# Phase 1 of a quantized feed-forward kernel: x turned on VectorE in 32x32 squares instead of on TensorE

## What is computed

```python
x: (4, 1024, 512)    cond: (4, 256)    W: (1536, 512)    w1: (2048, 512)    w2: (512, 2048)
hidden   = concat([cond, cond], -1)
fused    = concat([x, mean(x, axis=1) * ones, hidden * ones], -1)       # (4, 1024, 1536)
relation = relu(einsum('bld,do->blo', fused, W) + b)
def quant_linear(v, w, bias):
    s_in = max(max(v), 1e-8) / 255;             vq = clip(round(v / s_in), 0, 255) * s_in
    s_w  = max(max|w| per row, 1e-8) / 127;     wq = clip(round(w / s_w), -128, 127) * s_w
    return vq @ wq.T + round(bias / (s_in * s_w)) * (s_in * s_w)
h   = relu(quant_linear(relation, w1, b1))
out = x + quant_linear(h, w2, b2)
```

## Time and profile before

| | us |
|---|---|
| median of 3 runs | 348.81 (348.67 to 349.97) |
| the profiled execution | 349.05 |
| its span, first to last instruction | 346.8 |
| phase 1, to the first product of phase 2 | 0 to 117.5 |
| phase 2 | 117.5 to about 229 |
| phase 3 | about 233 to 346.8 |

### The profile page before, as it was taken

The page is one execution under the profiler, slowest core; times in us unless marked ns, Lnnn a source line. Parts: engine busy times, 40 slices in busy tenths (PEclk is TensorE's granted clock), DMA queues, the critical chain, the costliest instruction groups (busy, mean ns, idle before and its releaser), DMA issues.

```text
span 346.8 us, 5358 instructions
## 1 busy us (share of the span) xinstructions
PE 337.3 (97%) x1645; PEld 196.2 (57%) x1645; DVE 271.4 (78%) x590; ACT 155.7 (45%) x263; POOL 1.1 (0%) x8
## 2 busy tenths in 40 slices
PE   6999999999999999999999999989999999999996
PEld 5788888888868544444444444434444444444444
DVE  1877668658684789999999999988486595685996
ACT  2635225325412499970000000038959559568800
POOL 1000000000000000000000000000000000000000
PEclk9999999999999999999999999999999999999999
DMA  7965998964432128886781030037984399977116
GB/s 247 404 214 171 325 326 241 285 188 177 121 60 41 21 122 363 346 347 287 323 335 60 0 121 0 0 121 289 402 341 183 133 412 424 361 241 227 78 60 242
DMA packets 29934, 74.90 MB, mean 216 GB/s; under 512 B 17864, under 2 KB 18144, under 8 KB 22496
## 3 DMA queue, kind: packets, MB, share of 16 engines
q1 hardware_dynamic: 29920, 74.73, 59.7%
HBM read 45.37 MB, written 25.17 MB: 203 GB/s over the span
## 4 chain that ended last, share of the span: by engine, by line
PE 90%; DVE 4%; issue 3%; DMA 2%; SPq 0%; ACT 0%; DVEq 0%
PE bank L480 28%; PE bank L436 26%; PE bank L360 25%; PE bank L501 4%; PE bank L348 4%; DMA x_in<-in_x_dram 2%; PE bank L453 1%; DVE hidden L781 1%; DVE x_lo L618 1%; PE bank L448 1%; PE bank L399 1%; DVE steps L842 0%; DVE cw_lo L656 0%; PE bank L418 0%; SPq L225 0%
## 5 line engine op out<-in xcount | busy, mean ns | idle before, releaser
L436 PE MATMUL bank<-pool_r,w_t 128*128 (+1 forms) x480 | 103.8, 379 | 0.0
L781 DVE TENSOR_SCALAR_CACHE_REDUCE hidden<-bank,qb,hmax 128x512 f32 x128 | 97.6, 808 | 5.3 <-DVE hidden L781 1.5
L576 ACT ACTIVATE steps<-hidden,s_quant 128x512 int16 (+1 forms) x124 | 76.8, 708 | 21.1 <-DVE w_t L809 11.2
L436 PEld LDWEIGHTS bank<-pool_r,w_t 128*128 128x128 bf16 x480 | 47.0, 98 | 56.6
L480 PE MATMUL bank<-w_t 128*128 128x512 bf16 x256 | 56.2, 379 | 0.9 <-DVE w_t L844 0.9
L360 PE MATMUL bank<-x_hi,cw_hi 128*128 128x512 f32 x128 | 51.0, 398 | 0.8 <-issue 0.5
L360 PE MATMUL bank<-x_hi,cw_lo 128*128 128x512 f32 x128 | 49.9, 390 | 0.0
L360 PE MATMUL bank<-x_lo,cw_hi 128*128 128x512 f32 x128 | 49.9, 390 | 0.0
L623 DVE TENSOR_SCALAR_CACHE_REDUCE hidden<-bank 128x512 f32 (+1 forms) x31 | 21.3, 689 | 27.9 <-PE bank L360 27.9
L480 PEld LDWEIGHTS bank<-w_t 128*128 128x128 bf16 x256 | 24.8, 98 | 31.7 <-DVE w_t L844 1.5
L480 PE MATMUL bank<-w_t,pool_q 128*128 128x512 bf16 x192 | 41.9, 379 | 0.0
(11 more groups left out here) (101 smaller groups left out, 244.7 us busy)
## 6 DMA issues: line engine op xcount, KB each, us to landing
hidden_spill<-hidden SPq DMA_DIRECT2D x16, 1024.0 KB, 3.9
hidden<-hidden_spill SPq DMA_DIRECT2D x16, 1024.0 KB, 7.7
pool_q<-in_L_ffn_w_dram SPq DMA_DIRECT2D x8, 1024.0 KB, 5.5
pool_r<-in_x_dram SPq DMA_DIRECT2D x8, 1024.0 KB, 5.6
x_in<-in_x_dram SPq DMA_DIRECT2D x7, 1024.0 KB, 5.6
out_dram<-pool_r SPq DMA_DIRECT2D x7, 1024.0 KB, 4.2
pool_r<-in_L_cond_W_dram SPq DMA_DIRECT2D x1, 2048.0 KB, 11.0
x_in<-in_x_dram SPq DMA_DIRECT2D x2, 512.0 KB, 5.4
```

The costliest lines, as they stand in the source:

```text
L436: mm = pe.matmul(bank[ft % BANKS][:, :], w1_t[:, ft, k, :], act_q[:, bass.ds(n * (KD * TB) + k * TB, TB)], start=(k == 0), stop=(k == KD - 1))
L576: ins = act.activation(steps[:, q % 2, f, :], hidden[:, bass.ds(slot * HB + ft * TB, TB)], ACT.Copy, scale=s_quant[:, ft:ft + 1])
L781: dve.tensor_scalar(hidden[:, bass.ds(slot * HB + ft * TB, TB)], bank[ft % BANKS][:, :], qb1[:, ft:ft + 1], hmax[:, ft:ft + 1], ALU.add, A ...
```

## The change

- x is stored and loaded with 128 tokens next to each other on the partitions. From block 2 on it is loaded as pieces of 512 bytes, so that partition 32c + i holds feature group c of every 32nd token (`x_squares`; four DMAs a block).
- Block 0 and block 1 are still turned by PE, reading every fourth element. From block 2 on DVE turns x: four `dve.transpose` of 128x512 f32 a block, each of 16 squares of 32x32, read at a step of four elements, into one SBUF buffer `x_t`. ACT reads `x_t` instead of PSUM; the remainder is subtracted by POOL.
- The first-third rows of W are loaded in the order that goes with it (row 4p + k), by ACT's DMA queue.
- `REL` has four banks instead of two. Block 0's products are done by depth: for each `k` all four `ot`, in the order that the parts come ready.
- The int8 to bf16 cast of the weights moves from DVE to ACT, with two buffers.
- Order on DVE: `turn_x(n + 1)`, three `take_relation`, `scale_w(n)`, (the means), the fourth `take_relation`. `scale_w(0)` is in block 1, behind `turn_x(2)`.
- Phase 1's loops are written out. Stores and reloads of x have pieces of 2 KB instead of 8 KB.

```diff
-            x_in = sb("x_in", [P, 2, TJ, D], F32, first)
+            x_in = sb("x_in", [P, 2, TJ * D], F32, first)
+    x_squares = x.rearrange("b s d -> (b s) d").rearrange("(n q i) (c e) -> n c i q e", q=TQ, i=R, c=CG)
+    cw_turned = cond_w.rearrange("(g p k) o -> g p k o", p=P, k=KD)
+        x_t = raw[:, (NB - 1) * KD * TB:NB * KD * TB].rearrange("p (k t) -> p k t", k=KD)
-        REL = bank[4:6]
+        REL = bank[4:8]
...
 SP:
             def load_x(n, par):
+                for c in range(CG):
+                    sp.dma_start(x_in[c * R:(c + 1) * R, par, :].rearrange("i (q e) -> i q e", q=TQ),
+                                 x_squares[n, c, :, :, :]).then_inc(x_landed[par], 16)
...
+            for j in range(TJ):
+                sp.dma_start(x_in[:, 0, j * D:(j + 1) * D], x_blocks[0, :, j, :]).then_inc(x0_landed[j], 16)
+            sp.dma_start(x_in[:, 1, :].rearrange("p (j d) -> p j d", d=D), x_blocks[1]).then_inc(x_landed[1], 16)
             load_w(w1_chunks, 0, 0)
...
+            sp.wait_ge(x_turned, KD)
+            load_x(2, 0)
+            load_w(w1_chunks, 1, 1)
+            for n in range(NB):
+                if n + 3 < NB:
+                    sp.wait_ge(x_turned, KD * (n + 2))
+                    load_x(n + 3, (n + 1) % 2)
+                if n + 2 < NB:
+                    sp.wait_ge(w_steps_ready, 4 * (n + 1))
+                    ...                                   # load_w of chunk n + 2
+                turn_w(n)
...
 POOL:
+            for n in range(2, NB):
+                for k in range(KD):
+                    pool.wait_ge(hi_ready, KD * n + k + 1)
+                    pool.tensor_tensor(x_lo[:, n % 2, k, :], x_t[:, k, :], x_hi[:, n % 2, k, :].bitcast(F32),
+                                       ALU.subtract).then_inc(lo_ready, 1)
...
 PE:
+            def relation(n, ot):
+                pe.wait_ge(rel_taken, KD * (n - 1) + ot + 1)
...
+            for k in range(KD - 1):
+                pe.wait_ge(cw_hi_ready, k + 1)
+                pe.wait_ge(hi_ready, k + 1)
+                for ot in range(KD):
+                    product(0, k, ot, cw_hi, x_hi)
+                pe.wait_ge(cw_lo_ready, k + 1)
+                for ot in range(KD):
+                    product(0, k, ot, cw_lo, x_hi)
+                pe.wait_ge(lo_ready, k + 1)
+                for ot in range(KD):
+                    product(0, k, ot, cw_hi, x_lo)
...
+            for ot in range(KD):
+                product(0, k, ot, cw_hi, x_lo)
+                product(0, k, ot, cw_lo, x_hi).then_inc(rel_done, 1)
+                if ot == 0:
+                    pe.wait_ge(x_landed[1], 16)
+                    pe.wait_ge(cols_taken, 1)
+                    for kk in range(KD):
+                        for j in range(TJ):
+                            mm = turned_by_pe(1, j, kk)
+                        mm.then_inc(x_turned, 1)
+            for n in range(1, NB - 1):
+                for ot in range(KD):
+                    relation(n, ot)
...
 ACT:
+            def quantize_w(n, w2_rows):
+                act.wait_ge(winv_ready, n + 1)
+                ...                                       # four pieces to int8, as before
+                act.wait_ge(w_steps_ready, 4 * (n + 1))
+                if n >= 2:
+                    act.wait_ge(w_turned[n % 2], 16 * (n // 2))
+                act.activation(w_bf[n % 2], w_steps, ACT.Copy).then_inc(w_bf_ready, 1)
+            for k in range(KD):
+                act.dma_start(cw_in[:, k, :], cw_turned[0, :, k, :]).then_inc(cw_landed[k], 16)
...
+            for n in range(NB):
                 if n + 1 < NB:
+                    for k in range(KD):
+                        take_hi(n + 1, k)
+                quantize_w(n, n >= KD)
...
 DVE:
+            def turn_x(n):
+                dve.wait_ge(x_landed[n % 2], 16 * (CG * (n // 2) + n % 2))
+                dve.wait_ge(rel_done, KD * (n - 1))
+                squares = x_in[:, n % 2, :].rearrange("p (q r k) -> p k q r", q=TQ, k=KD)
+                for k in range(KD):
+                    if n > 2:
+                        dve.wait_ge(lo_ready, KD * (n - 1) + k + 1)
+                    dve.transpose(x_t[:, k, :].rearrange("p (q i) -> p q i", i=R),
+                                  squares[:, k, :, :]).then_inc(x_turned, 1)
...
+            for ot in range(KD):
+                take_relation(0, ot)
+                take_lo(1, ot)
+            for n in range(1, NB - 1):
+                turn_x(n + 1)
+                if n == 1:
+                    scale_w(0, False)
+                for ot in range(KD - 1):
+                    take_relation(n, ot)
+                scale_w(n, n >= KD)
+                if n == NB - 2:
+                    ...                                   # the means, as before
+                take_relation(n, KD - 1)
```

309 lines of the change are left out of this document (119 added, 190 removed).

## The result

| | before | after |
|---|---|---|
| median | 348.74 | 355.44 (4 runs, 351.99 to 356.61) |
| ratio | | 1.0167, interval 1.0094 to 1.0241 |
| the profiled execution / its span | 349.05 / 346.8 | 355.4 / 353.6 |
| first product of phase 2 | 117.55 | 124.65 |
| from there to the end of the span | 229.25 | 228.95 |

The forecast was 343.7 us, range 341.0 to 351.0: it missed. Phases 2 and 3 kept their time, so all of it is in phase 1, which was to be 5.1 us shorter and is 7.1 us longer. In a later set of ten runs the same kernel took 350.41 us (348.91 to 353.59, e5_after_again), so the size of its loss varies. The first product of phase 2 stands about 229 us ahead of the end of the span in every trace; its position therefore says how long the one profiled execution was, and no more than that.

What follows compares the result with a forecast made beforehand. The prediction took PE, busy for 97% of the span, as the bound. It summed -10.5 (transposes) - 1.45 (start) + 1.2 (block 1) + 4.6 (block 2) + 1.1 (means) = -5.1 us, giving 343.7 us, range 341.0 to 351.0.

Steps and rivals of the forecast that it cites:

- costed at zero: Loads of x in the loop: four DMAs a block on SP would land in time and add 0 us.
- the 1.1 I had: Block 6 to 7: PE's bias products wait for the means, now behind `scale_w(6)`; cost 1.1 us.
- Rival 5: New queues hold the turn 1 to 2 us in several blocks, such as late x: 347 to 352 us, chance 0.07.
- The start: landing: Block 0: x, sharing with W, lands at 8.5 us (bounds 7.5 to 9.6); the start as a whole gains 1.45 us.
- rival 3: PE's clock falls in block 2 after its waits, 2.7 us more for a quarter block: 346.4 us, chance 0.13.
- T: Price of one DVE transpose of 128x512 f32: 0.682 us taken as value and lower bound, upper bound 1.36.
- rival 1: DVE and PE reads at a step are slow, a DVE transpose taking 1.36 us: 349.8 us in all, chance 0.12.
- block 2's wait: PE waits 3.0 us for block 2's first remainder; block 2 costs 4.6 us in all.
- P: Price of one POOL subtraction of 128x512 (the remainder): 1.2 us taken, bounds 0.9 and 2.35.
- rival 2: POOL is the bound and the kernel gets slower, 2.35 us a subtraction: 353.7 us, chance 0.13.
- block 1's alternation: DVE alternates takes of block 0 with remainders of block 1, 1.3 us a pair; costs PE 1.2 us.
- the loop with slack: Steady blocks: the DVE, ACT, POOL, PE loop has 1.9 us slack at P = 1.2, so blocks run at 10.9 us.

Runs made afterwards that it cites:

- e5_after_again: The changed kernel (after), unchanged, run again on another chip: 350.41 us, ratio 1.0049 to before.
- e7: e1 plus more filler products in block 0 and ACT holding back W's chunks 1 to 3 until x of block 0 has nearly landed: 349.57 us, ratio 1.0016.
- e1: After, with SP issuing the loads of x(n + 4) ahead of the DMA transpose of chunk n: 348.65 us, ratio 0.9994.
- e13: After plus four corrections (x issued early, more fillers, block 2's high parts first, means first), x's four loads all on SP: 347.33 us, ratio 0.9953.
- e10: The four corrections of e13 on after, with x's four loads split between SP's and ACT's queues: 340.92 us, ratio 0.9775.
- e14: After, with only x's four loads a block split, two issued by SP and two by ACT: 350.19 us, ratio 1.0038.
- e2: After, with x of blocks 2 to 7 loaded in 2 KB instead of 512-byte pieces (values not the reference's): 349.19 us, ratio 1.0009.
- e16: e13 with x's four loads issued in the partition order 0, 2, 1, 3: 346.51 us, ratio 0.9935.
- e17: e13 with all four loads of x issued on ACT's queue, none on SP's: 340.43 us, ratio 0.9747.
- e9: After, with x of blocks 2 to 7 loaded by one DMA over 128 partitions, 512-byte pieces (values not the reference's): 348.98 us, ratio 0.9998.
- e3: After, with DVE's turn reading neighbouring elements instead of every fourth (values not the reference's): 347.38 us, ratio 0.9964.
- e11: The four corrections of e13 on after, with x loaded by the one wide DMA of e9 (values not the reference's): 340.52 us, ratio 0.9761.

## Why the prediction was wrong, point by point

1. **DMAs "costed at zero": the step that failed most.** I took x's issue at "about 9 us into block n, or at the worst 15", and its landing 5.6 us later, with "twice that still fits". The load for block 6 was issued 11.6 to 13.8 us into block 3 (at 68.10 to 70.33, block 3 starts at 56.5), inside those bounds, but it landed 12.60 us after its last issue. The load for block 7 was issued 18.2 us into block 4 (at 85.65, block 4 starts at 67.4), behind a DMA transpose of 9.16, and landed 9.16 us after its last issue. So both the landing and the issue left the bounds. In this trace that is 4.7 us of PE's waiting ahead of the bias products beyond the 1.1 I had, and 1.5 more by the low clock there. The earlier trace rows held the warning: SP held for 8.93 us by one DMA transpose. I read it as a delay that happens once. In after these issues last 3.6 to 9.2 us in the loop. Rival 5 named this, at 0.07 and with at most 352 us. That the kernel could be slower I gave 0.17, but 0.13 of it for POOL, which was not the reason.
2. **The start: landing.** 8.5 assumed, 10.4 measured (bounds 7.5 to 9.6): 1.9 us. W and x shared the DMA engines at 402 and 394 GB/s from 8 to 10 us, while only one of W's four chunks was wanted first. With three chunks held back x landed at 7.5 (e7), so it was W's bytes that delayed it.
3. **The start: the clock, not in the sum.** I looked for a fallen clock only in block 2 (rival 3), where it did fall (0.51 from 44 to 47 us) and cost nothing, since PE waited for each remainder anyway. It also fell at 10 us, behind waits of PE of about 1 us with three fillers in each, which cost 2.4 us in this trace (0 to 1.3 in the others), and at the bias products. The traces with more fillers show the first, e1 the second.
4. **T: size wrong, rival 1 right in its mechanism.** 1.08 instead of 0.68; block 2's wait was 4.02 instead of 3.0, and the first tile of block 2 ended 8.5 us behind block 1 (39.83 to 48.33) instead of 7.3, so 1.2 us, P's 0.09 included. A transpose over 1 us was one of my signs of being wrong, and it showed. In the steady blocks it fitted: 4.05 for the turn, 3.1 and 2.65 as before are 9.8 of 10.9 us.
5. **What held.** Six turns taken from PE, 10.5 us: blocks of 10.9 us without a PE wait in after. The remainders' price (1.29 against 1.2; rival 2 fell), the cast, block 1's alternation, the loop with slack, ACT's own queue ahead of x_hi of block 2. Phases 2 and 3 unchanged.

The sum: 1.9 + 2.4 + 1.2 + 4.7 + 1.5 = 11.7 of the 12.2 us between 112.45 and 124.65. It accounts for the profiled execution, whose 355.4 us is near the median of the first runs; in e5's trace the wait ahead of the bias products is 3.0 us instead of 5.77, and the start's low clock cost 1.3 instead of 2.3.

The plan was worth more than I gave it. With the order on ACT and DVE mended, the 4.6 and 1.1 us that I had booked as the price of block 2 and the means are gone. What a sum of one wait after the other did not show is that the corrections behind e1 together bring 1.4 us (e13's 0.9953 against e1's 0.9994) as long as SP's list is longer than a block, and 6 us more once it is shorter (e10's 0.9775).

**What stays open.** Why a DMA transpose's issue lasts between 1.3 and 11.9 us was not tested, and with it whether SP's own time or its queue behind it is the bound. How much 512-byte pieces cost of their own behind the 32 partitions is not separated (274 to 330 GB/s against 393 with 8 KB). e14 fits neither theory cleanly.

## What to carry to other kernels

Add up each DMA queue's issues for one turn of the loop like an engine's work, with the longest issue in it; a queue whose list is longer than the turn can be the bound even when each wait in the chain is short and is put down to something else. When removing the waits that a chain names moves the time little, look for a serial list that all the late things pass, and move one class of items off it before blaming the bandwidth. Ask of every new wait on PE what the clock will be behind it.

## What the runs showed of the hardware

- Loads onto 32 partitions, one behind the other on one queue, ran at 164 to 219 GB/s with pieces of 512 bytes or 2 KB (e2, e5, e13, e16, e17, from 27 or 28 us on); one load onto 128 partitions ran at 274 to 330 with 512 bytes (e9) and at 393 with 8 KB (before).
- VectorE's turn of 128x512 f32 in 32x32 squares takes 684 ns dense (e3) and 1077 ns read at a step of 16 bytes (after).
- One DMA transpose of 128x2048 bf16 held SP for 1.7 to 8.9 us in before (median 2.3) and for 3.6 to 11.9 us in the loops of after, e10, e13 and e17. The DMA engines' share can stand at 0.95 for 110 us without being the bound: e17 (0.95) and e11 (0.82) take the same time, 340.4 and 340.5 us.
- Three fillers in each wait of the start left 36 products at 8.4 to 10.7 us, from one execution to the next; more of them held the products at 8.40 to 8.45 us in ten of eleven traces.
